# Eight mixed attention and feed-forward stages on one core: where splits, first scores and filler products stand in the two attentions

## What is computed

```
# 16 heads of 128                                # 32 heads of 8
q = rmsnorm(x @ Wq[h]) * gq                      q = rope(x @ Wq, pos); k = rope(ctx @ Wk, pos); v = ctx @ Wv
k = rmsnorm(ctx @ Wk[h]) * gk                    p = softmax(q k^T / sqrt(8))
p = softmax(q k^T / sqrt(128))                   out = (p @ v) @ Wout + bout
out = sum_h p @ (ctx @ Wv[h]) @ Wo[h]
```

## Time and profile before

| what | value |
|---|---|
| median of 3 runs | 1110.71 us (1105.49 to 1112.2) |
| the profiled execution's own time | 1110.76 us |
| its span in the trace | 1109.0 us |
| TensorE matmul busy | 850.5 us (77%) |
| VectorE busy | 741.6 us (67%) |
| ScalarE busy | 567.9 us (51%) |
| GpSimd busy | 406.2 us (37%) |

### The profile page before, as it was taken

The page is one execution under the profiler, slowest core; times in us unless marked ns, Lnnn a source line. Parts: engine busy times, 40 slices in busy tenths (PEclk is TensorE's granted clock), DMA queues, the critical chain, the costliest instruction groups (busy, mean ns, idle before and its releaser), DMA issues. The chain is left out here.

```text
span 1109.0 us, 16326 instructions
## 1 busy us (share of the span) xinstructions
PE 850.5 (77%) x5170; PEld 503.2 (45%) x5170; DVE 741.6 (67%) x1441; ACT 567.9 (51%) x1070; POOL 406.2 (37%) x332
## 2 busy tenths in 40 slices
PE   3356666979899999998597588998539999634477
PEld 1122223642477777776376452332416666422135
DVE  5799996879666676666788557994533333157785
ACT  3433342477677777776474365887304432123162
POOL 0476650047555555553231270000025665202122
PEclk8689998999999999999699597999759999856589
DMA  3222205600000000000000101400572333230001
GB/s 91 78 76 76 76 1 199 219 10 11 10 15 19 19 20 20 14 19 1 5 1 1 52 1 39 135 3 2 201 276 53 74 49 48 28 96 0 0 1 38
DMA packets 44330, 57.61 MB, mean 52 GB/s; under 512 B 5656, under 2 KB 35104, under 8 KB 44272
## 3 DMA queue, kind: packets, MB, share of 16 engines
q1 hardware_dynamic: 37776, 48.72, 13.1%
q0 software_dynamic: 4416, 6.03, 3.3%
q10 hardware_dynamic: 2080, 2.10, 0.5%
HBM read 50.29 MB, written 6.49 MB: 51 GB/s over the span
## 5 line engine op out<-in xcount | busy, mean ns | idle before, releaser
L1225 POOL TENSOR_TENSOR a_scratch<-a_scratch,a_inverse 128x512 f32<-128x512 f32 x64 | 66.6, 1041 | 117.8 <-DVE a_inverse L1357 117.8
L322 PE MATMUL bank<-ssm_seen,ident 128*128 128x512 f32 x128 | 63.6, 621 | 39.0 <-DVE ssm_seen L498 39.0
L424 POOL TENSOR_TENSOR ssm_drive<-ssm_du,ssm_b_row 128x1024 f32<-128x1024 f32 x32 | 75.2, 2352 | 33.4 <-DVE ssm_state L488 33.3
L2204 DVE TENSOR_REDUCE a_tops<-bank 128x4 f32<-128x1024 f32 x64 | 77.6, 1223 | 13.5 <-PE bank L1893 10.7
L2403 PE MATMUL bank<-wup,moe_xT 128*128 x184 | 84.9, 605 | 1.2 <-ACT moe_xT L2461 1.1
L390 ACT ACTIVATE bank<-ssm_delta,ssm_a_neg 128x510 f32<-128x510 f32 x64 | 44.1, 690 | 80.7 <-DVE ssm_state L488 77.7
L2633 DVE TENSOR_TENSOR moe_act_f<-bank,moe_silu 128x512 f32<-128x512 f32 x23 | 15.9, 692 | 96.0 <-ACT moe_silu L2468 84.2
L488 DVE TENSOR_TENSOR_SCAN ssm_state<-bank,ssm_drive 128x512 f32<-128x512 f32 x64 | 74.8, 1210 | 7.6 <-POOL ssm_drive L424 4.9
L2057 ACT ACTIVATE wup<-bank,a_exp_scale 128x1024 f32<-128x1024 f32 x64 | 71.1, 1114 | 16.9 <-PE bank L1916 16.8
L1144 ACT ACTIVATE a_scratch<-bank,a_bias,a_q_factor 128x256 f32<-128x256 f32 x128 | 71.1, 560 | 10.4 <-DVE a_bias L1344 10.1
L969 PE MATMUL bank<-keys,a_scratch 128*128 (+1 forms) x256 | 69.8, 396 | 0.7 <-DVE keys L1282 0.4
(11 more groups left out here) (477 smaller groups left out, 2190.4 us busy)
## 6 DMA issues: line engine op xcount, KB each, us to landing
ssm_b_row<-ssm_b_spill SPq DMA_DIRECT2D x16, 512.0 KB, 3.6
wup<-in_l_up_dram SPq DMA_DIRECT2D x8, 1024.0 KB, 8.6
a_wq_in<-in_l1x_q_dram SPq DMA_DIRECT2D x32, 128.0 KB, 2.1
wdn<-in_l_down_dram SPq DMA_DIRECT2D x8, 512.0 KB, 9.6
keys<-in_l1x_o_dram SPq DMA_DIRECT2D x1, 2048.0 KB, 12.7
X<-in_x_dram SPq DMA_DIRECT2D x1, 1024.0 KB
lora_raw<-in_l_gate_dram SPq DMA_DIRECT2D x1, 1024.0 KB, 8.3
lora_raw<-in_l_up_dram SPq DMA_DIRECT2D x1, 1024.0 KB, 10.3
```

The source lines that it names most:

```text
L322: last = pe.matmul(bank[:, 4 + 2 * k + h, :], core.ident[:, :], seen[:, k, h * HALF:(h + 1) * HALF], start=False, stop=m >= STEPS - CC, sk ...
L424: pool.tensor_tensor(drive[:, k, :], du[:, k, :], b_row[:, n % NROW, :], ALU.mult).then_inc(S["drive_ready"], 1)
L1225: pool.tensor_tensor(prob[:, j, :, :], prob[:, j, :, :], inverse[:, j, :].unsqueeze(2).to_broadcast([P, 2, SEQ]), ALU.mult).then_inc(S["p_ ...
L2204: dve.tensor_reduce(tops[:, f // 2 % 3, :, first:first + 2].rearrange("p q h -> p h q"), bank[:, at:at + 2, :].rearrange("p h (q n) -> p h ...
```

## The change

In the 16-head attention:
- SyncE loads the gains ahead of the query weights, and VectorE waits for them and multiplies them behind the layernorm instead of at the start.
- VectorE's rounding, the splits of c and of the first two query weights move from before the `vo_step` work into the pairs that follow: rounding behind pair 2, its second half behind pair 3, the query splits behind pair 4, one quarter of `vo_low` and the split of c behind pair 5, the second quarter behind pair 6, the third into `first_unit`, the fourth into unit 1.
- TensorE makes both first scores around the last pair's sums, ahead of the last spread; unit 0 is written out, with `keep_busy(6)` and `keep_busy(4)` (128x512 f16) around its first turn; the waits for `c_split` and for the first quarter of vo stand ahead of unit 1, the wait for all four behind it. The wait for the last `k_logs` is gone.

In the 32-head attention the first scores and the first search of step 4 come ahead of the second `turn_tops`; the six fillers behind it become four groups of four in steps 0 and 1.

```diff
+                sp.dma_start(gains[:, :], d["l1x_gains"]).then_inc(in_s, 16)
                 for p in range(2):
                     load_q(p, p)
-                sp.dma_start(gains[:, :], d["l1x_gains"]).then_inc(in_s, 16)
...
                 queries(0, 0, 0)
                 spread_of(PAIRS - 2)
-                sums_of(PAIRS - 1)
-                query_sums(0, 0)
-                spread_of(PAIRS - 1)
...
+                def keep_busy(n):
+                    for _ in range(n):
+                        pe.matmul(bank[:, 0, :], wk[:, 0, 0, :], ctxT[:, 0, 0:HALF], start=True, stop=True)
...
+                pe.wait_ge(S["key_ready"], 4)
                 pe.wait_ge(S["k_brought"], 4 * PAIRS)
-                pe.wait_ge(S["k_logs"], PAIRS)
+                scores(0, 0, 0, 0)
+                sums_of(PAIRS - 1)
+                scores(0, 0, 0, 1)
+                query_sums(0, 0)
+                spread_of(PAIRS - 1)
+                turn_factor(0, 0)
+                queries(1, 0, 1)
+                pe.wait_ge(S["key_ready"], 4 * PAIRS - 3)
+                keep_busy(6)
+                turn(0, 0)
+                keep_busy(4)
+                query_sums(1, 1)
                 pe.wait_ge(S["c_split"], 1)
-                unit(0, 0, 0, None, 0)
                 pe.wait_ge(S["key_ready"], 4 * PAIRS)
+                pe.wait_ge(S["vo_split"], 1)
+                unit(1, 0, 1, 0, 0)
                 pe.wait_ge(S["vo_split"], 4)
-                unit(1, 0, 1, 0, 0)
...
-                dve.wait_ge(in_s, 16)
-                dve.tensor_tensor(gain[:, :], gains[:, 0:1], gains[:, 1:2], ALU.mult).then_inc(S["gain_done"], 1)
...
                 s.norm_vector(dve)
+                dve.wait_ge(in_s, 16)
+                dve.tensor_tensor(gain[:, :], gains[:, 0:1], gains[:, 1:2], ALU.mult).then_inc(S["gain_done"], 1)
...
                 for j in range(4):
                     scale_keys(1, j)
-                dve.tensor_scalar(core.raw_in, core.raw_in, ROUND, 1.0, ALU.subtract, ALU.min).then_inc(S["rounded"], 1)
-                dve.wait_ge(S["c_hi"], 1)
-                lower(c_flat, core.ctx_nat, 1, 0, S["c_split"])
-                for p in range(2):
-                    query_low(p, p)
                 dve.wait_ge(S["vo_sum"], 1)
...
                     if g == 2:
+                        dve.tensor_scalar(core.raw_in, core.raw_in, ROUND, 1.0, ALU.subtract, ALU.min).then_inc(S["rounded"], 1)
+                    if g == 3:
                         dve.wait_ge(S["rounded"], 1)
                         dve.tensor_scalar(core.tern[2][:, :], core.raw_in, -1.0, None, ALU.max).then_inc(S["tern_done"], 1)
-                    else:
-                        vo_low(g - 3)
+                    if g == 4:
+                        for p in range(2):
+                            query_low(p, p)
+                    if g == 5:
+                        vo_low(0)
+                        dve.wait_ge(S["c_hi"], 1)
+                        lower(c_flat, core.ctx_nat, 1, 0, S["c_split"])
+                    if g == 6:
+                        vo_low(1)
...
                     scale_keys(PAIRS - 1, 1)
+                    vo_low(2)
                     invert(0, 1)
...
                     mix_low(n - 1, 1)
+                    if isinstance(n, int) and n == 1:
+                        vo_low(3)
                     invert(n, 1)
...
-                turn_tops(1)
-                keep_busy(6, 5)
                 for f in range(NSTEP):
...
                         find_pair(f + AHEAD, 0)
+                    if f == 0:
+                        turn_tops(1)
+                    if f < 2:
+                        keep_busy(4, 6)
...
                         find_pair(f + AHEAD, 1)
+                    if f < 2:
+                        keep_busy(4, 6)
```

13 lines of the change are left out of this document (5 added, 8 removed).

## The result

| | before | after |
|---|---|---|
| median of 4 runs each | 1110.38 us (1105.49 to 1112.20) | 1097.06 us (1096.71 to 1098.76) |
| ratio | | 0.9879, 95% interval 0.985 to 0.9909 |
| the profiled execution, its span | 1110.76, 1109.0 us | 1098.76, 1097.0 us |

A forecast was written before the change was run, and what follows sets the result against it. No engine was taken to fill the span; stages have different limits, TensorE in the 16-head loop. Terms 2.8 + 3.9 + 1.2 - 0.3 - 0.3 + 4.8 = 12.1 us off 1110.76 gave 1098.7 us, range 1093 to 1105.

The forecast's parts named there:

- Part 1: 16-head start: gains loaded first, multiplied later, remove TensorE's idle time before the first key product; 2.8 us saved.
- Part 2: 16-head pairs: moving VectorE's early pieces to later pairs removes the stall before the fourth key sums; 3.9 us saved.
- what is late next?: 16-head later pairs: VectorE 0 to 1.5 us late after pair 6's scaling; GpSimd's last square at 278.2 to 279.3, hidden.
- Part 3: 16-head hand-over: scores ahead of the last sums bring unit 1's scores forward; 1.2 us saved beyond the 3.9 counted.
- the fillers cost nothing: 16-head hand-over: ten full-clock fillers of 0.22 us each delay nothing, since unit 1 waits until 289.0 anyway.
- rival B: 16-head hand-over: VectorE becomes the bound, collisions 1.5 us, half-clock fillers 1 to 2; 1101.7 us, chance 0.13.
- The fourth vo split: 16-head unit 1: VectorE's last split of vo stands ahead of a reciprocal; 0.3 us lost, bounds 0 and 1.3.
- Part 4, order: 32-head opening: scores come first, but fillers hand the head start back by step 2; 0.3 us lost.
- Part 4, clock: 32-head opening: fillers hold TensorE's full clock, so six exponentials take 8.93, not 13.71 us; 4.8 us saved.
- A: 32-head opening: the clock falls all the same and some fillers run at half clock; 1103.8 us, chance 0.20.
- C: 32-head opening keeps its 1.2 us head start, nothing collides, next stages gain a little; about 1096 us, chance 0.11.
- D: Late stages, 1000 to 1050: short bursts no longer lift the clock; about 1111 to 1113 us, chance 0.04.

The follow-up runs named there:

- e1: Kernel before with only the gains loaded first and multiplied behind the layernorm: 1112.59 us, ratio 1.0014.
- e2: Kernel before with gains first and VectorE's pieces in later pairs, TensorE's hand-over in the old order: 1106.90 us, ratio 0.9964.
- e11: As e2, plus ten full-size fillers: six ahead of the last sums, four ahead of the last spread: 1105.38 us, ratio 0.9942.
- e4: Kernel before with only the 32-head attention changed, 16-head code as before: 1104.46 us, ratio 0.9937.
- e7: Changed kernel without the ten fillers of the 16-head hand-over: 1099.01 us, ratio 0.9851.
- e8: Changed kernel with the wait for all four vo quarters moved from ahead of unit 2 into the output products: 1100.53 us, ratio 0.9854.
- e9: As e8, plus six fillers ahead of the first turned maxima in the 32-head searches: 1096.82 us, ratio 0.9854.
- e3: Kernel before with the whole 16-head change, 32-head attention as before: 1107.87 us, ratio 0.9964.

## Why the prediction came out right

- **Part 1, 2.8 us:** 2.95, kept through all spreads. Right, and by the mechanism named. What the text didn't say: alone it shortens the stage by 1.6 against before and the kernel by nothing that can be measured (e1).
- **Part 2, 3.9 us:** 34.48 - 29.47 in e2 and in all later ones, against 8.93: 3.92. Right for the stall. The question "what is late next?" was answered with VectorE (0 to 1.5 us; it was 0.5) and GpSimd (last square "278.2 to 279.3", hidden). With TensorE's old order the answer would have been wrong: the gap ahead of the last sums grew from 0.63 to 1.61 us, and the moved pieces cost 1.62 us over the hand-over at full clock (e11 against e4) and 2.83 more at half clock (e2 against e11). In the changed kernel the first scores fill this gap.
- **Part 3, 1.2 us:** 12.41 us from the seventh spread to unit 1 against 13.80 in the trace of before: 1.39. The chain came out nearly step by step, but the size is in part luck. The text counted from a hand-over with its last spread at half clock (2.00 us), and the same code at full clock takes 12.14 us (e4): against that execution the new hand-over is 0.27 us slower. At full clock throughout, the moved pieces cost 1.62 and the order gives 1.35 back; the rest of the 1.39 is the 1.66 us of half clock that before had and e4 had not. From the key product to unit 1, parts 2 and 3 together are 5.31 us against before (5.1 was forecast) and 3.54 against e4. That "the fillers cost nothing" held to 0.01 us at unit 1; that they gain 1.8 us (e7, one execution) was not in the sum. The remark on rival B, that TensorE has no long gap in which to lose its clock, held with the fillers in; in e7, without them, the clock fell.
- **The fourth vo split, 0.3 us:** 0.71. This term was mis-sized, and for another reason than given: the text asked about the reciprocal behind it, and the price was TensorE's wait for all four quarters ahead of unit 2 (e8 removes 0.74, and e9, with the same edit, 0.73).
- **Part 4, order, a loss of 0.3:** with the clock equal, step 2's first exponential comes 0.2 us earlier (16.64 against 16.84). The 1.33 us lost in the first trace of the changed kernel were a dip in the searches that its repeat doesn't have.
- **Part 4, clock, 4.8 us:** 13.71 to 8.94 is 4.77. Right as a difference between these two executions. But the term rested on one execution of the old opening, and this varies: the stage took 171.5, 173.5, 173.6, 178.2 and 179.3 us. What the fillers buy is 2 to 12 us by the moment (167.7 to 169.3 with them, seven executions). They seem to buy steadiness too: ten executions of e4, with them, lie between 1102.75 and 1105.99 us, ten of e3, without them, between 1100.95 and 1116.49.
- **Rivals.** A: the clock stayed at 1.00 in all seven openings with the sixteen fillers, and fell in all without. B: 0.5 us of its 1.5, no filler at half clock. C: of the head start of 1.2 us it reckons with, 0.2 was left in the repeat by step 2, and nothing in the first trace. D: the late stretch is at 0.60, as before.
- **The sum** was 12.1 us for the profiled execution, and the two profiled executions lie 12.0 apart. It was right by more than its due: two of its terms, the 1.2 us of part 3 and the 4.8 us of part 4, are differences from one execution of code whose clock differs from execution to execution. Singly the two halves give ratios of 0.9964 and 0.9937, product 0.990; together 0.9879 and 0.9865. The product lies inside the first interval (0.985 to 0.9909) and at the edge of the second (0.9829 to 0.9901), so the times do not show that the halves depend on one another. The stage lengths show that what the 16-head part wins can be lost again in the old 32-head opening (e3), and in seven executions with its fillers in it was not.

Open: what tips the clock in the first 5 us of the 16-head stage, at the old hand-over, and in the searches. No run here sets it; the same code gave 0.66 and 1.00 in the first place, a last spread of 2.00 and of 1.14 us in the second, and 0.68 and 1.00 in the third.

## What to carry to other kernels

A stall that is removed can come back as a gap somewhere, and if TensorE has only small products around that gap, the gap can cost more than itself: here 1 us more idle went with 2.8 us of half clock. Look for where TensorE will wait next and put full-size products there if nothing useful fits; they are free in idle time. And when a term of the sum is a clock term, one execution is one draw: look for the same code in other executions, also in those variants that were built for something else, before sizing it, and compare stages from their own start, with the granted clock beside them.

## What the runs showed of the hardware

- TensorE stayed at 0.50 for 30 us with 5.00 of 5 us busy in every stretch (e3, 674 to 704), with searches and scores of 32 rows, weighted values of nine columns and transposes. In the same opening sixteen 128x512 products held 1.00 with TensorE busy 4.70 of 5 us (after, 670 to 675).
- Identical code: 1.00 or 0.66 in the first 5 us of a stage, worth 1.69 us each time; with equal clock, times 60 us into the stage agree to 0.02 us between kernels with the same code up to there.
- The same old hand-over, with idle gaps of 0.6 and 1.0 us each time: the clock fell in two executions (last spread 2.00 and 2.09 us) and stayed at 1.00 in a third (1.14 us), which is worth 1.66 us.
- Unchanged stages vary too: the ternary one took 83.45 us with 15.6 us at half clock and 86.52 with 24.6. The time at half clock is not all of it, since in e11 the stage took 85.23 us with 13.7.
- A 128x1024 split on VectorE took 1.28 us alone and 1.49, 1.54, 1.64 or 2.06 beside GpSimd's work; two query splits 1.86 and 2.43. What a move costs depends on what it lands beside, which the sum had as a range and not as one price.
